# Moving the residual sum and layer norm one group later in the front of a fused decoder kernel

## What is computed

```python
x = _layernorm(x + attn(x))        # RMS norm, one head, rotary embedding, softmax, projection
x = _layernorm(x + xattn(ctx, x))  # 16 heads of 64; ctx: 16 x 1444 x 128; both sides layer-normed,
                                   # q = ln(x) @ Wq scaled and shifted per batch and head,
                                   # k, v = split(ln(ctx) @ Wkv); softmax(q k) v; @ Wout
x = _layernorm(x + ffn(x))         # product keys: top 8 of 8 x 8, 1024 experts
```

## Time and profile before

| | |
|---|---|
| time of the kernel before, median of 3 runs | 1323.63 us (1322.28 to 1325.7) |
| profiled execution, its own time | 1320.99 us |
| profiled execution, span | 1319.3 us |
| mean granted TensorE clock over the span | 0.904 of full |
| end of the front (last `w2h` copy ends) | 93.77 us into the span |
| busy over the span | PE 1168.6, DVE 1133.0, ACT 890.4, POOL 621.4 us |

### The profile page before, as it was taken

The page is one execution under the profiler, slowest core; times in us unless marked ns, Lnnn a source line. Parts: engine busy times, 40 slices in busy tenths (PEclk is TensorE's granted clock), DMA queues, the critical chain, the costliest instruction groups (busy, mean ns, idle before and its releaser), DMA issues. The chain is left out here.

```text
span 1319.3 us, 32707 instructions
## 1 busy us (share of the span) xinstructions
PE 1168.6 (89%) x12762; PEld 909.4 (69%) x12762; DVE 1133.0 (86%) x2847; ACT 890.4 (67%) x1260; POOL 621.4 (47%) x520
## 2 busy tenths in 40 slices
PE   6778999999999999999999999999997839877778
PEld 4655676767777777777777767677776727767678
DVE  6547998999989899998999999898986688999984
ACT  5559788888888888888889878888884332212121
POOL 3215757577575667757567675667330310000000
PEclk9679999999999999999999999999999766556666
DMA  8107999999999999999999999999998300000000
GB/s 173 24 24 148 184 197 194 195 192 194 191 188 199 202 192 198 197 198 196 191 197 190 196 190 195 185 188 185 180 187 135 105 0 2 5 5 6 5 5 6
DMA packets 665392, 186.25 MB, mean 141 GB/s; under 512 B 653938, under 2 KB 662294, under 8 KB 664854
## 3 DMA queue, kind: packets, MB, share of 16 engines
q1 hardware_dynamic: 665238, 184.16, 81.1%
HBM read 19.97 MB, written 0.82 MB: 16 GB/s over the span
## 5 line engine op out<-in xcount | busy, mean ns | idle before, releaser
L1169 PE MATMUL ps<-pT,xa_hi 128*128 128x128 f16 x2288 | 381.2, 217 | 26.3 <-DMA pT<-p 25.9
L978 ACT ACTIVATE e<-ps,bias 128x1444 f32<-128x1444 f32 (+1 forms) x208 | 305.4, 1468 | 126.5 <-DVE bias L1051 125.2
L1165 PE MATMUL ps<-pT,xa_hi 128*128 128x128 f16 x2288 | 383.1, 217 | 6.3 <-ACT uT L1001 5.6
L1166 PE MATMUL ps<-pT,xa_lo 128*128 128x128 f16 x2288 | 383.1, 217 | 0.0
L1049 DVE TENSOR_REDUCE nmax<-ps 128x1 f32<-128x1444 f32 (+1 forms) x208 | 344.0, 1654 | 33.3 <-PE ps L1149 32.8
L1061 DVE TENSOR_TENSOR p<-e,p 128x1408 f16<-128x1408 f32 (+3 forms) x288 | 303.5, 1095 | 31.5 <-ACT p L986 30.4
L986 ACT ACTIVATE p<-e 128x1408 f16<-128x1408 f32 (+1 forms) x208 | 288.2, 1386 | 13.3
L934 POOL TENSOR_TENSOR p<-e,p 128x1408 f16<-128x1408 f32 (+1 forms) x128 | 196.6, 1557 | 181.6 <-ACT p L986 181.6
L1169 PEld LDWEIGHTS ps<-pT,xa_hi 128*128 128x128 f16 x2288 | 222.0, 98 | 33.9 <-DMA pT<-p 33.6
L1165 PEld LDWEIGHTS ps<-pT,xa_hi 128*128 128x128 f16 x2288 | 222.2, 98 | 30.0 <-issue 15.1
L1147 PE MATMUL ps<-xT_hi,q_hi 128*128 128x512 f16 (+1 forms) x624 | 229.0, 367 | 5.0 <-POOL q_lo L923 3.2
(11 more groups left out here) (235 smaller groups left out, 1938.8 us busy)
## 6 DMA issues: line engine op xcount, KB each, us to landing
raw<-in_ctx SPq DMA_DIRECT2D x16, 704.0 KB
pT<-p SPq DMA_TRANSPOSE x416, 4.2
f_wq<-in_L_ffn_w_q SPq DMA_DIRECT2D x1, 1024.0 KB, 5.0
f_wqt<-in_ffn_wq_t SPq DMA_DIRECT2D x2, 512.0 KB, 6.7
raw<-in_ctx SPq DMA_DIRECT2D x48, 18.0 KB
x_tok<-in_x SPq DMA_DIRECT2D x4, 200.0 KB
out_x<-ost SPq DMA_DIRECT2D x6, 128.0 KB, 2.0
wk_t<-in_wk_t SPq DMA_DIRECT2D x1, 512.0 KB, 10.0
```

The costliest lines, as they stand in the source:

```text
L978: act.activation(e32[t % E_BUF][rows, :], score_banks(t)[rows, 0:T], ACT.Exp, bias=bias[rows, t % N_BUF:t % N_BUF + 1]).then_inc(e_done, 1)
L1165: pe.matmul(out, hi, ph, start=n == 0, stop=False)
L1166: pe.matmul(out, lo, ph, start=False, stop=False)
L1169: pe.matmul(out, hi, pl, start=False, stop=False)
```

## The change

Four things are changed.

1. In every engine's list of the front the part from `stats` on (`stats`, `norm_rstd`, `shifts`, `twice_normed`, `once_normed`, `ln_turned`, `queries_out`, `queries_hi`, `queries_lo`) stands about one group later against the attention part. On PE `scores(c)` moves ahead of `projected(c - 1)`'s place in the list, and `queries_keys` of the group after next ahead of `weighted`.
2. The fold products are spread between other steps: `qa_lo_out(k)` on DVE and `qa_hi_out(k)` on ACT no longer stand together, and `values_with_out(k)` is a function with the same four products as before.
3. `context_norm_act` is cut in three parts of four tiles, put between `exponents` and the copies. On POOL `context_lo` now stands ahead of all four `norm_rstd`.
4. The norm of batch 1's context at the start of `cross` is 12 DVE instructions (`context_norm` ahead of `maximum(0)`) in place of 12 on ACT; `context_shift(second)` is dropped and `crn` needs one buffer.

```diff
@@ gpsimd
             context_rstd(pool, cx, nhalf, first)
+            context_lo(pool, cx, first)
             norm_rstd(0)
-            context_lo(pool, cx, first)
             norm_rstd(1)
             norm_rstd(2)
+            norm_rstd(3)
             context_rstd(pool, cx, nhalf, second)
-            norm_rstd(3)
@@ scalar
             v_out(0)
             exponents(0)
+            v_out(1)
             probT_out(0)
-            v_out(1)
             oT_out(0)
-            context_norm_act(act, cx, first)
+            context_norm_act(act, cx, first, 0)
             exponents(1)
+            context_norm_act(act, cx, first, 1)
+            v_out(2)
+            probT_out(1)
+            oT_out(1)
+            context_norm_act(act, cx, first, 2)
+            exponents(2)
+            context_hi(act, cx, first)
+            v_out(3)
+            probT_out(2)
+            oT_out(2)
             twice_normed(0)
-            context_hi(act, cx, first)
-            probT_out(1)
-            v_out(2)
-            oT_out(1)
+            exponents(3)
             once_normed(0)
-            exponents(2)
-            twice_normed(1)
-            queries_hi(0)
-            probT_out(2)
-            v_out(3)
-            oT_out(2)
-            once_normed(1)
-            exponents(3)
             prod_out(0)
             prod_out(1)
-            twice_normed(2)
-            queries_hi(1)
             probT_out(3)
+            queries_hi(0)
+            twice_normed(1)
             prod_out(2)
             oT_out(3)
             prod_out(3)
-            for k in range(NG):
-                qa_hi_out(k)
+            once_normed(1)
+            qa_hi_out(0)
+            qa_hi_out(1)
+            queries_hi(1)
+            twice_normed(2)
+            qa_hi_out(2)
+            qa_hi_out(3)
+            act.wait_ge(wvo_ps, 1)
+            act.activation(prod[:, of(0), :], bank(4, D, (4, D)), ACT.Copy).then_inc(wvo_done, 1)
             queries_hi(2)
             twice_normed(3)
...
@@ vector
             weights(0)
+            rotated(1, 1)
             context_shift(dve, cx, first)
-            rotated(1, 1)
             doubled(2)
             doubled(3)
-            stats(0)
             maxima(1)
             rotated(2, 0)
-            shifts(0)
             weights(1)
             rotated(2, 1)
-            queries_out(0)
-            stats(1)
+            stats(0)
             maxima(2)
             rotated(3, 0)
-            shifts(1)
             weights(2)
             rotated(3, 1)
+            shifts(0)
+            stats(1)
+            maxima(3)
+            context_mix(dve, cx, first)
+            queries_out(0)
+            weights(3)
+            shifts(1)
+            stats(2)
             queries_lo(0)
             queries_out(1)
-            context_mix(dve, cx, first)
-            stats(2)
-            maxima(3)
             dve.wait_ge(ld_k, LD_K)
             dve.tensor_reduce(ksum[:, :], wk_d[:, :, :], AX_X, ALU.add).then_inc(ksum_done, 1)
             shifts(2)
-            weights(3)
+            qa_lo_out(0)
             queries_lo(1)
+            stats(3)
+            qa_lo_out(1)
             queries_out(2)
-            stats(3)
+            qa_lo_out(2)
+            shifts(3)
+            qa_lo_out(3)
+            queries_lo(2)
             for part in range(4):
                 context_stats(dve, cx, second, part)
-            for k in range(NG):
-                qa_lo_out(k)
-            shifts(3)
-            queries_lo(2)
             for k in range(2, NG):
                 dve.wait_ge(wvo_ps, k + 1)
                 dve.tensor_copy(prod[:, of(k), :], bank(4 + k, D, (4, D))).then_inc(wvo_done, 1)
             queries_out(3)
             queries_lo(3)
-            context_shift(dve, cx, second)
@@ tensor
             values(0)
+            turned_x(3)
             queries_keys(1, 0)
-            turned_x(3)
             scores(0)
             queries_keys(1, 1)
             values(1)
             prob_turned(0)
+            queries_keys(2, 0)
             weighted(0)
-            queries_keys(2, 0)
+            scores(1)
             pe.wait_ge(ld_late, LD_LATE)
             projected(0)
-            scores(1)
             queries_keys(2, 1)
             values(2)
             prob_turned(1)
-            ln_turned(0)
+            queries_keys(3, 0)
             weighted(1)
-            queries_keys(3, 0)
+            scores(2)
             projected(1)
-            scores(2)
             queries_keys(3, 1)
             values(3)
             prob_turned(2)
-            ln_turned(1)
-            weighted(2)
             pe.wait_ge(ld_k, LD_K)
             keys_with_queries(0)
-            projected(2)
+            weighted(2)
             scores(3)
             keys_with_queries(1)
+            projected(2)
+            ln_turned(0)
             keys_with_queries(2)
+            prob_turned(3)
             keys_with_queries(3)
-            prob_turned(3)
-            ln_turned(2)
+            weighted(3)
+            ln_turned(1)
             pe.wait_ge(fold_done, 5)
             keys_folded(0)
-            weighted(3)
+            projected(3)
             keys_folded(1)
             keys_folded(2)
-            projected(3)
             keys_folded(3)
+            ln_turned(2)
             pe.wait_ge(ld_v, LD_V)
             for k in range(NG):
-                pe.wait_ge(qa_lo_done, k + 1)
...
+                values_with_out(k)
             ln_turned(3)
@@ cross
...
-            context_norm_act(act, cx, Batch(None, 1))
...
+            for part in range(3):
+                context_norm(dve, cx, Batch(None, 1), part)
             for t in range(ALL_TILES + DRAIN):
```

More of the change, by code:

```diff
@@ L276, in _ @@
             prod_out(3)
-            for k in range(NG):
-                qa_hi_out(k)
+            once_normed(1)
[7 more added lines that the diff above has]
+            act.activation(prod[:, of(0), :], bank(4, D, (4, D)), ACT.Copy).then_inc(wvo_done, 1)
             queries_hi(2)
             twice_normed(3)
-            for k in range(2):
-                act.wait_ge(wvo_ps, k + 1)
-                act.activation(prod[:, of(k), :], bank(4 + k, D, (4, D)), ACT.Copy).then_inc(wvo_done, 1)
+            act.wait_ge(wvo_ps, 2)
+            act.activation(prod[:, of(1), :], bank(5, D, (4, D)), ACT.Copy).then_inc(wvo_done, 1)
+            once_normed(2)
             queries_hi(3)
-            once_normed(2)
             once_normed(3)
@@ L503, in keys_folded, with values_with_out @@
                 last.then_inc(qa_ps, 1)
+            def values_with_out(k):
+                pe.wait_ge(qa_lo_done, k + 1)
+                for j in range(4):
+                    last = pe.matmul(bank(4 + k, D, (4, D))[:, j, :], wv_t[:, 4 * k + j, :], wout[:, 4 * k + j, :], start=True, stop=True)
+                last.then_inc(wvo_ps, 1)
             pe.wait_ge(const_chain, 3)
@@ L534, in _ @@
             prob_turned(2)
-            ln_turned(1)
-            weighted(2)
             pe.wait_ge(ld_k, LD_K)
             keys_with_queries(0)
-            projected(2)
+            weighted(2)
             scores(3)
             keys_with_queries(1)
+            projected(2)
+            ln_turned(0)
             keys_with_queries(2)
+            prob_turned(3)
             keys_with_queries(3)
-            prob_turned(3)
-            ln_turned(2)
+            weighted(3)
+            ln_turned(1)
             pe.wait_ge(fold_done, 5)
             keys_folded(0)
-            weighted(3)
+            projected(3)
             keys_folded(1)
             keys_folded(2)
-            projected(3)
             keys_folded(3)
+            ln_turned(2)
             pe.wait_ge(ld_v, LD_V)
             for k in range(NG):
-                pe.wait_ge(qa_lo_done, k + 1)
-                for j in range(4):
-                    last = pe.matmul(bank(4 + k, D, (4, D))[:, j, :], wv_t[:, 4 * k + j, :], wout[:, 4 * k + j, :], start=True, stop=True)
-                last.then_inc(wvo_ps, 1)
+                values_with_out(k)
             ln_turned(3)
@@ L606, in __init__ @@
         self.lo_rows = sb("lo_rows", [P, 1])
-        self.crn = [sb(f"crn{i}", [P, NTILE]) for i in range(2)]
+        self.crn = sb("crn", [P, NTILE])
         self.xT_hi = [sb(f"xT_hi{i}", [D, PW], F16) for i in range(2)]
@@ L689, in context_shift, with context_norm_act @@
     dve.wait_ge(c.ctx_rstd, bt.val(1, 1))
-    dve.scalar_tensor_tensor(out=c.crn[bt.par][:, :], in0=c.cmv[bt.par][:, :, 0], scalar=-1.0, in1=c.crs[bt.par][:, :],
+    dve.scalar_tensor_tensor(out=c.crn[:, :], in0=c.cmv[bt.par][:, :, 0], scalar=-1.0, in1=c.crs[bt.par][:, :],
                              op0=ALU.mult, op1=ALU.mult).then_inc(c.crn_done, 1)
-def context_norm_act(act, c, bt):
-    act.wait_ge(c.crn_done, bt.val(1, 1))
-    if bt.off >= 1:
-        act.wait_ge(c.xa_lo_done, bt.val(1, 0))
-        act.wait_ge(c.xa_mix_done, bt.val(1, 0))
-    for n in range(NTILE):
+def context_norm_act(act, c, bt, part):
```

(8 more changed lines are left out.)

## The result

| | before | after |
|---|---|---|
| median of the comparison | 1322.95 us (1320.02 to 1325.70, 4 runs) | 1300.42 us (1297.89 to 1301.83, 4 runs) |
| profiled execution, own time | 1320.99 us | 1300.68 us |
| its span | 1319.3 us | 1299.0 us |
| end of the front | 93.77 us | 77.74 us |

The ratio is 0.9833 with an interval of 0.9813 to 0.9853: 22.5 us are gained, where 14.6 were forecast.

What follows compares the result with a forecast made beforehand. The front was taken as one chain ending at 93.77 us, with TensorE at 1.2 GHz the bound in one stretch; ending it at 79.1 gains 14.7, start of `cross` 0, so 1323.63 - 14.6 = 1309.0 us, range 1304.5 to 1314.5.

Steps and rivals of the forecast that it cites:

- if `cross` keeps its pace: Condition on the front: it is one chain, so shortening it shortens the time provided `cross` runs as before; no size given.
- Start of cross: First steps of `cross`: removing ACT's 12 activations gains 0, DVE's 12 instructions fit; 0 taken, bounds 0 and +1 us.
- the joint: Between front and `cross`: `exponent(0)` 8.9 us behind the last `w2h` copy, as before; growth would show the forecast wrong.
- (d): Rival, better: `kT` not held, clock back early each time; front ends at 77.0, total 1306 to 1303 us; chance 0.10.
- The ring: Front's attention turns, group by group: 7.4 us instead of about 13; `prob` ends near 24.8, 32.1, 39.5 and 51.1.
- The new wait: Group 3: DVE's `shifts(0)` waits for POOL's `norm_rstd(0)`, now queued behind `context_lo`; price 3.7 us.
- the hold of `kT`: Group 3: DVE's last `rotated(3,1)` instruction held beside POOL's `xa_lo`; without it the sum would be some 1 us better.
- The tail: Front behind the last group: no 5.7 us gap before L557; front ends at 79.1 against 93.77 us.
- (b): Rival, slower: TensorE at 1.2 GHz from group 1 to the front's end; total 1328 us; chance 0.02.
- (c): Rival, nothing gained: the layer norm only trails the ring and POOL's wait eats all; total 1323 us; chance 0.02.
- (a): Rival: TensorE at the low clock for one or two stretches forecast as fast, costing 2 to 6 us; 1311 to 1317; chance 0.22.

Runs made afterwards that it cites:

- e10: Changed kernel with residual sum and statistics back in the ring for groups 1 to 3 (PE and DVE lists): 1305.28 us, ratio 0.9892 to the kernel before.
- e3: Changed kernel with `norm_rstd(0)` ahead of `context_lo` in POOL's list: 1299.23 us, ratio 0.9839 to the kernel before.
- e9: Changed kernel with `context_lo` behind `norm_rstd(0)` to `norm_rstd(2)` in POOL's list: 1295.23 us, ratio 0.9805 to the kernel before.
- e8: Changed kernel with `context_lo` behind `norm_rstd(0)` and `norm_rstd(1)` in POOL's list: 1297.65 us, ratio 0.9830 to the kernel before.
- e7: Changed kernel with the four `qa_lo_out` together behind the second batch's context statistics again: 1303.29 us, ratio 0.9876 to the kernel before.
- e1: Changed kernel with an unused tile giving back the 64 bytes, so later tiles lie as before: 1307.29 us, ratio 0.9895 to the kernel before.
- e5: Changed kernel with `pT` alone moved 64 bytes later: 1297.94 us, ratio 0.9834 to the kernel before.
- e6: Changed kernel with `p` 64 bytes later and `pT` at a multiple of 256: 1304.10 us, ratio 0.9873 to the kernel before.
- e11: Changed kernel with 128 unused bytes ahead of `p`: 1304.31 us, ratio 0.9888 to the kernel before.
- e13: Changed kernel with 256 unused bytes ahead of `p`: 1300.06 us, ratio 0.9833 to the kernel before.
- the repetition: The changed kernel run again with no edit: 1302.49 us, ratio 0.9853 to the kernel before.
- e4: Changed kernel with the context norm of batch 1 on ACT again and `context_shift` back on DVE: 1302.28 us, ratio 0.9861 to the kernel before.
- e2: Kernel before with one `crn` buffer in place of two and nothing reordered: 1314.80 us, ratio 0.9949 to the kernel before.

## Why the prediction missed

**The step that failed** is the premise "if `cross` keeps its pace". Under *Start of cross* the sum prices the instructions that go with the second buffer of `crn`, but the buffer itself, 64 bytes ahead of every later tile, has no term: it was put at nothing without a reason. It is worth 5.1 us between the exponentials of the two profiles, and 4.8 to 6.6 us by the times (the pairs above; 6.2 between the means of the two groups). No row of the kernel before could give the price: its transposes took 1.7 us throughout, in the median, with nothing to compare. What could have been seen is that `p0` starts 64 past a multiple of 256 and that the change moves it there by exactly 64, while PE waits 25.9 us for what is read from it. That would have been worth a rival. With `p` at its old place the changed kernel's order gives 1 - 0.9885, 15.2 us, against the 14.6 forecast, and 1304.1 to 1307.3 us in the three kernels. In the profiles the forecast has a span of 1304.7 us and the kernel took 1299.0: of these 5.7 us the pace of `cross` is 5.1, the front 1.4 and the part behind the last exponential 0.2, and the joint takes 1.0 back. No rival had `cross` in it, and the measured time lies below the best of (d) too.

**The ring.** Right. `prob` at 31.97, 39.09 and 50.16 us against 32.1, 39.5 and 51.1; the clock at 1.00 from 24 to 44. e10 shows that `projected` and the statistics in the ring cost 3 us a turn.

**The new wait and the hold of `kT`.** Both are there (DVE idle 1.53 us until `rstd`; `kT` 3.03 us). Their prices were the wrong way round. The wait of 3.7 us is worth 0.35 us of front (e3), and the hold, "some 1 us", is the larger: with `context_lo` out of the ring, and with it both, the last turn is 3.7 us shorter and the front 2.8 (e9); from e3, where the wait is gone already, to e9 it is 2.4. That the last turn came out near the forecast all the same (11.07 us against 11.6) is luck: together the two are worth 3.7 us of that turn where the forecast has 4.2, but one price was far too high and the other too low. I had not seen that the hold can reach a small instruction behind `kT` as well, as `nb` in e8.

**The tail.** The gap before the products with `wout` is gone and was worth 5.2 us (e7). The front ends at 77.74 us in place of 79.1. Of these 1.4 us, 0.9 were there at `prob` of group 3 (50.16 against 51.1), and at the last `keys_folded` all of them (61.6 against 63.0). In the other kernels whose front is as changed (e1, e5, e6, e11, e13 and the repetition) it ended between 77.21 and 82.15.

**The joint.** The removal of ACT's 12 activations gains 0 and DVE's 12 instructions cost 0, as said (3.87 us, between the bounds of 2.4 and 4.8; e4). The joint is 1.0 us longer all the same, which the forecast had named as a sign of being wrong: of the bounds +1.8 and -1.5 for the clock I took 0, and the first scores, at 0.51, take 3.7 us from the first product to the end of the last, where they took 2.8 before.

**Rivals.** (b) and (c) did not come. (a), a low clock in places of the ring, is what the repetition, e13 and e9 show for one turn, at 1.7, 1.7 and 1.5 us. (d) without the hold is e9: its front of 75.0 us is 2.0 below the end that I gave it.

**Slips in the sums.** None moves the result. The tail gives 14.7 us and the sum carries 14.6. In (b), 99.1 against 93.77 makes 1329, not 1328, and the stretch from 24.8 to 94.0 is 69.2 us long. `projected` "at the high clock", 1.10 us, starts before the clock is back at 44.3 us; in the changed kernel it takes 0.92. The 3.78 and 1.73 us in the earlier trace rows are each two instructions merged, of 1408 and 36 columns, and not one difference.

Not settled: which moves carry the remaining 5.7 us of the front, why PE's idle time before the first `prob_turned` differs from run to run, and how `nb` came to be held in e8.

## What to carry to other kernels

Before a change is costed, look at which SBUF tiles it makes, drops or resizes: where a tile that a DMA transpose reads comes to lie past a multiple of 256 bytes can be worth as much as an edit of the schedule (6 us here, against 5 for the tail). An unused tile of the right size ahead of it should set it right; the runs show the tile moved off such a multiple by unused tiles and onto it by a dropped buffer (e2), but none pads a slow place to a fast one. Work that only trails a ring (here a residual sum and its statistics) belongs behind the next turn's start on every engine's list (e10), and a long POOL instruction that nothing in the ring needs behind the ring altogether (e9). A wait that a profile shows is worth only what the next-latest input leaves of it: 3.7 us on one engine were 0.35 us of the end.

## What the runs showed of the hardware

- DMA transposes from SBUF to SBUF of fp16 blocks keep the issuing queue for 1.44 to 1.46 us (high parts; low parts 1.44 to 1.45) and land in 3.7 us where the tile read starts at a multiple of 256 bytes, and 1.72 to 1.74 (1.67 to 1.68) and 4.1 to 4.2 us at 64 or 128 past one (before, after, e1, e2, e5, e6, e11, e13). The start of the written tile, 64 past, makes no difference (e5).
- A DVE instruction on four numbers per partition, 0.17 us by itself, took 4.28 us beside two POOL instructions back to back, and ended with the second (e8); beside the first of them alone it took 0.17 (e9). The Trainium skill, page "SBUF — State Buffer", section "Who interferes with whom", has an exclusion between DVE and GpSimd for a whole instruction, and for a `tensor_scalar` such as this one only in a two-port mode; no run shows which mode it was in, and the section says nothing of two GpSimd instructions in a row.
- The same list of instructions, run again, had TensorE's clock fall in another place: fronts between 77.21 and 82.15 us in the seven profiles of kernels that differ only in where tiles lie or not at all. In one turn the fall came behind an idle time of PE of 2.49 to 2.57 us and did not come behind 1.86 to 2.31 us (fourteen profiles of the changed order and its variants).
